# Roots by Newton steps on VectorE instead of GpSimd, expert blocks in groups of three pairs and one, the last pair's scatters two behind each send

## What is computed

```
x = x + stack(_layernorm(x))        # 8 layers, then a layer norm with gf, bef
x = x + moe(_layernorm(x))

# moe(x), E = 8, K = 2, H = 512, TEMP = 1.5
xn = (x - mu) * rsqrt(var + EPS) * gamma + beta
probs = softmax((xn @ router_w.T) / TEMP)
w, idx = top_k(probs, 2)
h = silu(xn @ W1[e]);  y = h @ W2[e]        # for the chosen experts e
out = sum over the two of w * y, + x
```

## Time and profile before

| | |
|---|---|
| runs | 1108.13, 1108.31, 1109.04 us, median 1108.31 |
| the profiled execution | 1106.82 us, its span 1105.1 us |
| TensorE matmul busy | 1013.6 us (92%) |
| VectorE, ScalarE, GpSimd busy | 764.8 (69%), 836.1 (76%), 797.6 us (72%) |
| GpSimd's scatters (L786) | 64, 63.1 us busy, mean 987 ns |
| mean granted TensorE clock | 0.969 |

### The profile page before, as it was taken

The page is one execution under the profiler, slowest core; times in us unless marked ns, Lnnn a source line. Parts: engine busy times, 40 slices in busy tenths (PEclk is TensorE's granted clock), DMA queues, the critical chain, the costliest instruction groups (busy, mean ns, idle before and its releaser), DMA issues.

```text
span 1105.1 us, 25020 instructions
## 1 busy us (share of the span) xinstructions
PE 1013.6 (92%) x7766; PEld 953.6 (86%) x7766; DVE 764.8 (69%) x2706; ACT 836.1 (76%) x1621; POOL 797.6 (72%) x1207
## 2 busy tenths in 40 slices
PE   5899899999999999999999999999998648897993
PEld 4798899999999999999999999999998648897992
DVE  6767577777777777777777777777789876443124
ACT  6777688888888888888888888888887637464572
POOL 5958867677767767776777677766777777777772
PEclk9999899999999999999999999999999859999997
DMA  4100010080008003500530080007002145754685
GB/s 135 49 1 16 20 49 1 15 153 24 1 18 165 11 4 66 115 10 15 98 81 1 15 147 31 1 16 150 11 1 59 57 136 178 198 160 144 210 243 170
DMA packets 85154, 82.24 MB, mean 74 GB/s; under 512 B 6779, under 2 KB 65791, under 8 KB 85024
## 3 DMA queue, kind: packets, MB, share of 16 engines
q1 hardware_dynamic: 80480, 72.18, 26.6%
q0 software_dynamic: 4544, 8.47, 2.2%
HBM read 45.15 MB, written 29.44 MB: 67 GB/s over the span
## 4 chain that ended last, share of the span: by engine, by line
PE 71%; DVE 8%; POOL 7%; issue 5%; ACT 4%; DMA 2%; SPq 2%; POOLq 0%; ACTq 0%; DVEq 0%
PE ps L1669 17%; PE ps L1557 8%; PE ps L1559 8%; PE ps L1558 8%; PE ps L1609 7%; PE ps L1603 6%; PE ps L1635 5%; PE ps L1834 4%; PE ps L1817 4%; PE ps L1591 2%; ACT s L895 2%; POOL xs L786 2%; DVE x_lo L1157 2%; DVE stat L1077 1%; DVE mv L1081 1%
## 5 line engine op out<-in xcount | busy, mean ns | idle before, releaser
L1669 PE MATMUL ps<-this_w,hid 128*128 128x128 f32 x2048 | 246.2, 276 | 0.0
L895 ACT ACTIVATE s<-s,shift,rstd 128x128 f32<-128x128 f32 x512 | 210.3, 485 | 45.1 <-POOL shift L606 44.1
L1669 PEld LDWEIGHTS ps<-this_w,hid 128*128 128x128 f32 x2048 | 237.9, 193 | 0.3 <-issue 0.2
L878 ACT ACTIVATE hid<-ps,col 128x512 f32<-128x512 f32 x256 | 155.4, 684 | 3.5 <-PE ps L1559 3.3
L604 POOL TENSOR_TENSOR rstd<-var,neg_half 128x4 f32<-128x4 f32 x136 | 148.6, 1093 | 11.3
L643 POOL TENSOR_TENSOR res_a<-s,row 128x512 f32<-128x512 f32 x60 | 76.8, 1280 | 73.0 <-ACT s L895 73.0
L1557 PE MATMUL ps<-x_hi,this_w 128*128 128x512 f32 x256 | 109.5, 428 | 3.1 <-DVE x_lo L1157 3.1
L601 POOL TENSOR_SCALAR shift<-mv 128x4 f32<-128x4 f32 x136 | 27.5, 202 | 115.2 <-DVE mv L1081 115.1
L1077 DVE BATCH_NORM_STATS2 stat<-s 128x6 f32<-128x128 f32 x512 | 110.1, 276 | 0.0
L1559 PE MATMUL ps<-x_hi,this_w 128*128 128x512 f32 x256 | 101.6, 397 | 0.0
L1558 PE MATMUL ps<-x_lo,this_w 128*128 128x512 f32 x256 | 101.3, 396 | 0.0
(11 more groups left out here) (217 smaller groups left out, 2726.6 us busy)
## 6 DMA issues: line engine op xcount, KB each, us to landing
xs<-pad SPq DMA_DIRECT2D x6, 2925.0 KB, 18.7
res_a<-w SPq DMA_DIRECT2D x39, 256.0 KB
xblk<-xs SPq DMA_DIRECT2D x78, 65.0 KB
raw_w<-w SPq DMA_DIRECT2D x18, 256.0 KB, 7.7
row<-rows SPq DMA_DIRECT2D x9, 512.0 KB, 4.8
this_w<-next_w SPq DMA_DIRECT2D x8, 512.0 KB, 3.2
this_qkv<-next_qkv SPq DMA_DIRECT2D x7, 384.0 KB, 2.6
scaled_w<-w SPq DMA_DIRECT2D x10, 256.0 KB
```

The lines of the kernel that those rows point to most:

```text
L878: a.activation(hid[h][:, c, :], ps(3 + h + c), ACT.Gelu, bias=col[:, bass.ds(lw * FF + (C_C1 + c), 1)]).then_inc(hid_done, 1)
L895: ins = a.activation(dst[:, t, :], src[:, t, :], ACT.Identity, bias=shift[i][:, t:t + 1], scale=rstd[i][:, t:t + 1])
L1669: ins = t_.matmul(ps(3 if h == 0 else 6)[:, t * P:(t + 1) * P], hid[h][:, c, t * P:(t + 1) * P], this_w2[:, c, :], start=c == 0, stop=c == ...
```

## The change

- The groups are now (0, 1, 2) and (3). The stages hold 9, 16, 30 and 23 blocks, 78 as before; the first block that needs pair 1, 2 or 3 is now block 9, 25 or 55. EARLY is six halves.
- The roots behind the stack move from GpSimd to VectorE: sum_inv of pairs 1 to 3, stack_inv of pairs 2 and 3, the last layer's last two inv_std2 (now last_inv), and keep_inv of all pairs. rsqrt makes a root from an integer start value and three Newton steps, ten chained instructions in place of one pow. With what stands around them these are 13, 11, 14 and 13 instructions a call, 141 in all.
- GpSimd does the 32 scatters of pairs 0 and 1 in one go, the 16 of pair 2 behind send 6, and of pair 3 two behind each of the sends 29 to 36.
- The steps of pairs 2 and 3 stand at other blocks on VectorE, ScalarE and TensorE. outer_residual(4) and (5) now stand ahead of block 0; table(0) stands behind routing(1); routing is cut in two halves; norm2 of the last pair moves from blocks 11 and 12 to 13 and 16.

The change's core (the new token_tiles and token_copy do what token_rows did, and first_choice and second_choice what routing did):

```diff
 
-GROUPS = ((0, 1), (2, 3))
+GROUPS = ((0, 1, 2), (3,))
...
 RING, YB, XROW = 8, 22, 4
+THIRD, THIRDS = 6, 16
+FOURTH, FOURTHS = 29, 2
 ENTRIES, LEAD = 4, 3
...
 BIG = 1e30
+RSQRT_START = float(0x5f3759df)
...
@@ -768,24 +772,18 @@
             for s in range(SLOTS):
                 slot(LAST, LAST % 2, s, False, True)
 
-            def keep_inv(p):
-
-                link(g.tensor_scalar(g_one[p][:, :], f_mv[1][p][:, :, 1], 1.0, EPS, ALU.mult, ALU.add))
-                link(g.tensor_tensor(g_std[p][:, :], g_one[p][:, :], half8[:, :], ALU.pow))
-                g.tensor_tensor(g_shift[p][:, :], g_std[p][:, :], g_neg[p][:, :], ALU.mult)
-                g.tensor_scalar(g_one[p][:, :], g_std[p][:, :], 1.0, 1.0, ALU.mult, ALU.add).then_inc(fin_ready, 1)
-
-            def scatter(u, k):
-
-                if u == 0 and k == 0:
-                    pool.wait_ge(filled, 16 * FILLS)
-                pool.wait_ge(slot_done, u // 2 + 1)
-                pool.wait_ge(xrow_done, u + 1)
-                for t in range(T):
-                    at = (u % 2) * T + t
-                    g.indirect_dma_start(
-                        out=xs, out_offset=bass.IndirectOffsetOnAxis(ap=slot_i[u // 2][:, k, at:at + 1], axis=0),
-                        in_=xrow[u % XROW][:, k, t, :], in_offset=None).then_inc(sent[u % XROW], 16)
+            def scatter(p, i):
+
+                u, k, t = 2 * p + i // (2 * T), i // T % 2, i % T
+                if t == 0:
+                    if u == 0 and k == 0:
+                        pool.wait_ge(filled, 16 * FILLS)
+                    pool.wait_ge(slot_done, p + 1)
+                    pool.wait_ge(xrow_done, u + 1)
+                at = (u % 2) * T + t
+                g.indirect_dma_start(
+                    out=xs, out_offset=bass.IndirectOffsetOnAxis(ap=slot_i[p][:, k, at:at + 1], axis=0),
+                    in_=xrow[u % XROW][:, k, t, :], in_offset=None).then_inc(sent[u % XROW], 16)
 
             def send_block(b):
 
...
             resid_f(LAST, 3, 1, LAST % 2)
             inv_std2(LAST, 2, 0)
             inv_std2(LAST, 2, 1)
-            scatter(0, 0)
-            scatter(0, 1)
-            sum_inv(1)
-            scatter(1, 0)
-            scatter(1, 1)
-            scatter(2, 0)
-            scatter(2, 1)
-            stack_inv(4)
-            stack_inv(5)
-            scatter(3, 0)
-            scatter(3, 1)
-            inv_std2(LAST, 3, 0)
-            sum_inv(2)
-            inv_std2(LAST, 3, 1)
+            for p in range(2):
+                for i in range(4 * T):
+                    scatter(p, i)
             for b in range(N_BLOCKS):
-                if b == 8:
-                    for u in (4, 5):
-                        scatter(u, 0)
-                        scatter(u, 1)
-                elif b == 14:
-                    stack_inv(6)
-                    stack_inv(7)
-                elif b == 22:
-                    sum_inv(3)
-                elif b == 33:
-                    for u in (6, 7):
-                        scatter(u, 0)
-                        scatter(u, 1)
-                elif b in (50, 53, 56, 59):
-                    keep_inv((b - 50) // 3)
                 send_block(b)
+                for p, first, per in ((2, THIRD, THIRDS), (3, FOURTH, FOURTHS)):
+                    if first <= b < first + 4 * T // per:
+                        for i in range(per):
+                            scatter(p, per * (b - first) + i)
 
 
         @block.scalar
...
             block_features(1)
             for b in range(N_BLOCKS):
                 silu(b)
-                if b in (11, 12):
-                    norm2(LAST, 3, b - 11)
                 if b + 2 < N_BLOCKS:
                     block_features(b + 2)
-                if b == 5:
+                if b == 1:
                     feature_rows(4)
                     feature_rows(5)
-                elif b == 8:
-                    token_rows(4)
-                elif b == 9:
+                elif b in (3, 5):
+                    token_rows(4 + b // 4)
+                elif b == 6:
                     exponentials(2)
-                elif b == 10:
-                    token_rows(5)
-                elif b == 29:
+                elif b in (13, 16):
+                    norm2(LAST, 3, (b - 13) // 3)
+                elif b == 28:
                     feature_rows(6)
                     feature_rows(7)
-                elif b == 31:
-                    token_rows(6)
+                elif b in (29, 31):
+                    token_rows(6 + b // 31)
                 elif b == 32:
-                    token_rows(7)
-                elif b == 34:
                     exponentials(3)
                 elif b in range(61, 61 + 2 * HALVES, 2):
                     keep_sum((b - 61) // 2)
...
 
+            def rsqrt(y, v):
+
+                n = v.shape[1]
+                link(d.tensor_scalar(y.bitcast(I32), v.bitcast(I32), -0.5, RSQRT_START, ALU.mult, ALU.add))
+                for _ in range(3):
+                    link(d.scalar_tensor_tensor(out=newton[:, 0:n], in0=v, scalar=-0.5, in1=y, op0=ALU.mult, op1=ALU.mult))
+                    link(d.tensor_tensor(newton[:, 0:n], newton[:, 0:n], y, ALU.mult))
+                    link(d.scalar_tensor_tensor(out=y, in0=newton[:, 0:n], scalar=1.5, in1=y, op0=ALU.add, op1=ALU.mult))
+
+            def last_inv(h):
+
+                i = 2 + h
+                dve.wait_ge(x2_done, upto(LAST, 2, h, base=8))
+                dve.wait_ge(mv2_done, upto(LAST, 3, h, base=8))
+                d.tensor_scalar(shift[i][:, :], mv[i][:, :, 0], -1.0, None, ALU.mult)
+                link(d.tensor_scalar(var[i][:, :], mv[i][:, :, 1], EPS, None, ALU.add))
+                rsqrt(rstd[i][:, :], var[i][:, :])
+                d.tensor_tensor(shift[i][:, :], shift[i][:, :], rstd[i][:, :], ALU.mult).then_inc(rstd2_done, 1)
+
+            def stack_inv(p):
+
+                dve.wait_ge(mv0_done, 2 * p + 2)
+                link(d.tensor_scalar(f_var[p][:, :], f_mv[0][p][:, :, 1], EPS, None, ALU.add))
+                rsqrt(f_std[p][:, :], f_var[p][:, :])
+
+            def sum_inv(p):
+
+                dve.wait_ge(mvg_done, 2 * p + 2)
+                d.tensor_scalar(g_neg[p][:, :], f_mv[1][p][:, :, 0], -1.0, None, ALU.mult)
+                link(d.tensor_scalar(n_var[p][:, :], f_mv[1][p][:, :, 1], 1.0 + EPS, EPS * EPS, ALU.mult, ALU.add))
+                rsqrt(n_std[p][:, :], n_var[p][:, :])
+                d.tensor_tensor(n_shift[p][:, :], n_std[p][:, :], g_neg[p][:, :], ALU.mult).then_inc(std_done, 1)
+
+            def keep_inv(p):
+
+                link(d.tensor_scalar(g_one[p][:, :], f_mv[1][p][:, :, 1], EPS, None, ALU.add))
+                rsqrt(g_std[p][:, :], g_one[p][:, :])
+                d.tensor_tensor(g_shift[p][:, :], g_std[p][:, :], g_neg[p][:, :], ALU.mult)
+                d.tensor_scalar(g_one[p][:, :], g_std[p][:, :], 1.0, None, ALU.add).then_inc(fin_ready, 1)
+
             def outer_residual(u):
 
                 p, at = u // 2, (u % 2) * T
-                dve.wait_ge(std0_done, u + 1)
+                if u < 4:
+                    dve.wait_ge(std0_done, u + 1)
                 dve.wait_ge(offset_done, u + 1)
                 for t in range(T):
                     ins = d.scalar_tensor_tensor(out=res_a[:, u, t, :], in0=res_a[:, u, t, :],
...
             outer_residual(3)
             sum_moments(2)
             sum_moments(3)
-            table(0)
+            sum_inv(1)
             logits(1)
             routing(1)
+            table(0)
+            slots(1)
+            weights(1)
             last_residual(4)
             last_residual(5)
-            slots(1)
-            weights(1)
+            add_res2(LAST, 3, 0, True)
+            add_res2(LAST, 3, 1, True)
             stack_moments(4)
             stack_moments(5)
-            add_res2(LAST, 3, 0, True)
-            add_res2(LAST, 3, 1, True)
+            stack_inv(2)
+            outer_residual(4)
+            outer_residual(5)
             table(1)
-            moments2(LAST, 3, 0)
-            moments2(LAST, 3, 1)
             for b in range(N_BLOCKS):
                 block_result(b)
-                if b in (1, 2):
-                    outer_residual(b + 3)
-                elif b in (3, 4):
-                    sum_moments(b + 1)
-                elif b == 7:
+                if b in (0, 1):
+                    sum_moments(4 + b)
+                elif b == 2:
+                    sum_inv(2)
+                elif b == 4:
                     logits(2)
+                elif b == 5:
+                    first_choice(2)
+                elif b == 6:
+                    second_choice(2)
                 elif b == 8:
-                    routing(2)
-                elif b == 10:
                     slots(2)
                     weights(2)
-                elif b == 11:
+                elif b == 9:
                     table(2)
-                elif b in (13, 14):
```

(45 more changed lines are left out.)

21 lines of the change are left out of this document (15 added, 6 removed).

## The result

The changed kernel takes **1102.4 us** (median of 5 runs, 1099.8 to 1103.8), the kernel before 1108.1 beside it: ratio 0.9945, 95% interval 0.9929 to 0.9961. In a later set of runs it took 1103.8 us, ratio 0.9962 (0.9950 to 0.9975). The prediction had 1089.3 and a range from 1082 to 1098. The sign was right, but two thirds of the gain are missing. The profiled execution took 1102.9 us, its span is 1101.1.

A forecast was written before the change was run, and what follows sets the result against it. TensorE was taken to set the pace, with winnable time where it is held. Ten steps summed to -19.0 us against the profiled 1106.8, giving 1087.8, plus 1.5 for the median: 1089.3 us, range 1082 to 1098.

The forecast's parts named there:

- Step 1: Block 0: sum_inv(1) leaves GpSimd, so the last scatter starts sooner, with weights in by 894; -2.8 us.
- Step 3: ScalarE: norm2 of the last pair moves to blocks 13 and 16; -1.0 us, bounds -3 and +2.
- Step 4: stack_inv(3) on VectorE: the wait for f_std on GpSimd and its slow clock go; -6.9 us.
- Step 5: Pair 3 needed at block 55, no longer 48: the old wait and its slow clock go; -8.0 us.
- Step 6: Pair 2 needed at block 25: scatters tie with TensorE, third block slightly late; +0.8 us, bounds 0 and +7.
- Step 7: New wait at block 55 for pair 3's scatters, 1.9 us, and 1.0 two blocks later; +2.9 us.
- Step 9: Six halves loaded early instead of four, costing SyncE time; +0.7 us, bounds 0 and 4.
- Step 10: Behind the last block, two halves are loaded and added, no longer four; -3.6 us.
- A: New hand-overs cost as before: block 25 or 55 waits 5 us; 1095 us, both 1100; chance 0.15.
- B: No new wait, and ScalarE's waits vanish too: 1083 us; chance 0.12.
- C: VectorE's small steps slow GpSimd's scatters and sends: 1118 us, slower than before; chance 0.03.
- D: GpSimd waits at send 29, shifting the same hold to block 55: 1094 to 1097 us; chance 0.12.

The follow-up runs named there:

- e6: Changed kernel with one Newton step instead of three in every root on VectorE: 1098.2 us, ratio 0.9919.
- r1b: Changed kernel with norm2 of the last pair at blocks 15 and 18 instead of 13 and 16, second run: 1102.0 us, ratio 0.9935.
- r2: Changed kernel with ScalarE's token rows of pairs 2 and 3 spread over two blocks each and the exponentials moved later: 1097.5 us, ratio 0.9913.
- e7: Changed kernel with pair 3's 16 scatters behind send 34 and the old groups (0, 1), (2, 3): 1104.7 us, ratio 0.9969.
- c1: Changed kernel with norm2 later, token rows and exponentials spread, early result loads behind the last block's load, pair 3's scatters behind send 34: 1085.9 us.
- r3: Changed kernel with the six early result loads issued behind the last block's load: 1101.7 us, ratio 0.9943.
- c2: c1 with table entries read ahead and all additions of loaded results behind result 77: 1082.8 us, ratio 0.9771.
- c3: c2 with table entries read ahead for pairs 1 to 3 only and the last two result loads ahead of four stores: 1080.3 us, ratio 0.9750.
- a0: Changed kernel unedited, run again beside the edits: 1103.8 us, ratio 0.9962 to the kernel before.
- f1: Changed kernel with norm2 of the last pair two blocks later and table entries of pairs 1 to 3 read ahead: 1092.8 us, ratio 0.9872.

## Why the prediction was wrong

Steps 1 to 10 against the leads of the first table:

- **Step 1**, -2.8: 1.8 at block 0. The block's load goes out at 892.10, 3.3 us sooner than in the earlier trace rows, but it and the block's weights are complete at 895.56 only, 3.5 us later, where it took 2.0 before. The first weights, behind table(0), go out at 890.44, as foretold. Both count on one semaphore, so which of them came last the trace doesn't tell; that both are in by 894 was the estimate that failed.
- **Step 2**, -1.1: the wait is gone, though the lead grows by 0.5 us only from block 0 to block 6.
- **Step 3 failed**: "Work moved, not removed: -1.0, bounds -3 and +2". Measured: +7.7 between blocks 6 and 20, far outside the bounds. The row was misread, too. Of the 3.6 us in five waits only 2.2 lie at blocks up to 12; 1.4 belong to the token rows of pair 3. The first and the last wait in the kernel before:
```profile
927.27 1.15 PE L1834 MATMUL ps<-heads,hid 128*128 x8 [0.54 <-ACT hid L1014]
...
989.07 1.15 PE L1834 MATMUL ps<-heads,hid 128*128 x8 [0.87 <-ACT hid L1014]
```
What I left out is when the input of ScalarE's work is there. Before, the moments of the last norm2 stand ahead of block 0's result and its roots ahead of GpSimd's first send, so that ScalarE finds them ready at blocks 11 and 12. The change puts moments, root and norm2 into three successive blocks, with a chain of 2.36 us on VectorE in the middle, and it puts token_rows right behind sum_inv(2). e6 shows that most of the waits come from there: 2.35, 2.20 and 2.22 us become 0.53, 1.02 and 1.03. r1b shows it for norm2, where both waits go. The 1.34 us behind the exponential are the amount of ScalarE's work in one place, which r2 spreads. The rule I broke was my own: an in-order queue that gets a new wait delays all that is queued behind it. I applied it to GpSimd and VectorE and not to ScalarE.
- **Step 4**, -6.9: 7.1. **Step 5**, -8.0: 8.2. Both hits, and e7 shows that step 5 belongs to the regrouping.
- **Step 6**, "A tie", +0.8: the changed kernel shows 0, but only because step 3's loss gave pair 2 its slack. It lies between result 8 and block 25, and there slips don't cancel. Where it is taken out, blocks 25 to 29 cost 5.7 us (r1b) and, with all four edits, 6.0 (c1), near the upper bound of +7. The tie itself was right: block 25 waits 0.36 (r1b) and 0.64 us (c1). The third block was mis-sized. Its load goes out 4.8 us behind the first, as worked out, but TensorE gets it 4.45 us later (960.27 to 964.72 in r1b) and not 2.0, a wait of 3.15 instead of 1.0, and from 965 to 967 us the granted clock is 0.51. So even with step 3 right, 1089 would not have come out.
- **Step 7**, +2.9: 4.2. The first part is close: the last scatter starts at 1023.73, the wait is 1.52, where 1.9 was worked out. The third block waits 2.06, not 1.0: its load (1031.33) takes 3.3 us to its transpose, not 2.0. The granted clock stays at 1.00 there. From the start of the last scatter to the load (1026.47) it is 2.7 us. The Trainium skill (DMA: Bandwidth & Descriptors, "Anatomy of one DMA") has about 2.0 for the fixed part of a DMA from GpSimd. This trace shows 0.7 more for a longer path, which ends with SyncE's issue, and it was the longer figure that gave the wait.
- **Step 8**, 0: right. GpSimd waits for results at the end.
- **Step 9**, +0.7 with an upper bound of 4: 3.9. It was mis-sized because I priced two more loads and not what all six pairs do to the block loads. r3 shows the size: without them among the blocks the last transpose comes 5.4 us sooner. Two causes are argued and not parted. One is SyncE's budget: it issues a DMA every 0.52 us, and every fourth block reads its table for about 3 us, 8 x 0.52 + 3 = 7.2 of the 7.6 us of four blocks, which leaves no room. It fits block 73, whose load goes out 6.3 us behind that of block 72. The other is the transfers: the DMA engines are busy 0.96 of the stretch, and block 72, whose load went out in time, came 6.3 us later.
- **Step 10**, -3.6: 2.4 from the last transpose to the end. Two additions behind the second are gone, as worked out, but the second (1097.25) is hardly sooner than in the earlier trace rows (1097.35), though the last transpose is 1.6 us sooner. Of that, 0.7 us lie ahead of the loads: the first goes out at 1090.02, in the earlier trace rows at 1090.98, behind stores that wait for VectorE. The rest lies between load and landing. From the last transpose to the end it is 23.8 us in c2 and 21.2 in c3, so the order of that queue is worth 2.6 us where the additions come late.

Of the rivals, A came nearest (1095 and 1100) by the wrong place: GpSimd's hand-overs, not ScalarE's. B supposed that ScalarE's waits vanish, and they trebled. C is refuted: the 64 scatters took 0.976 us on average, 0.987 before, and those beside a Newton chain (937.28, 938.54 and 939.80 beside that of 938.14) 0.96 each. So the rule of the Trainium skill that was cited for it (SBUF — State Buffer, "SBUF: two separate sides") shows no cost with these small steps. One scatter (890.53) took 1.46 us beside VectorE's 128x512 additions with two inputs. The small steps are 139, not 141: last_inv has 13. D is half true: half of the hold that left block 48 came back at blocks 55 to 58.

What stays open: the two shares in step 9, which a run with the loads' issues and not their bytes among the blocks would part. And the comparison of single traces has its limits. r1b is 3.6 us ahead of a0 at blocks 59 to 71, but only 0.5 ahead of the first trace of the changed kernel: a0 itself, the same code, falls 2.3 us behind that trace between blocks 56 and 59 and has 1.6 of them back by block 77.

## What to carry to other kernels

Where a computation is moved to another engine, look for its readers as well as its queue: how long before the read is the input ready now, and what stands behind the reader in its own queue. Waits that stand one behind another hide each other (r1b's 7.2 us at block 24 were 1.5 at block 29, f1's 8.1 still 7.5), so a repair that gains nothing in the time is judged by the lead at its own place. And an engine that only issues DMAs has a budget too: count its issues and register reads per block against the pace of the engine that it feeds.
